# The handoff from a graph attention layer's projection to its first round: scores of the last row tile from W times a, the largest score inside the projection, the first parts dealt anew

## What is computed

```python
h = relu(layernorm(x)); x = x + _L0_gnn_ref(h, adj, adj)     # smoothing with a normalised adjacency
h = relu(layernorm(x)); x = x + _L1_gnn_ref(h, adj, W, a1, a2, W1, b1, ..., W4, b4)

def _L1_gnn_ref(x, adj, W, a1, a2, ...):                     # 8 heads of 64 features
    Wh = jnp.einsum('nf,hfd->hnd', x, W)
    e_src = jnp.einsum('hnd,hd->hn', Wh, a1)
    e_dst = jnp.einsum('hnd,hd->hn', Wh, a2)
    e = jax.nn.leaky_relu(e_src[:, :, None] + e_dst[:, None, :], 0.2)
    e = jnp.where(adj[None] > 0, e, -9e15)
    h = jax.nn.elu(jnp.einsum('hnm,hmd->hnd', jax.nn.softmax(e, axis=-1), Wh))
    ...                                                      # four dense layers, the last without relu
```

## Time and profile before

| | us |
|---|---|
| median of 3 runs | 876.22 (873.47 to 876.56) |
| profiled execution | 876.4 |
| its span, first to last instruction | 874.3 |
| busy: PE / DVE / ACT / POOL | 844.2 / 701.2 / 426.6 / 280.0 |
| granted TensorE clock, mean | 0.993 of full |

### The profile page before, as it was taken

How to read it: one execution, slowest core, us unless ns; L and a number is a source line. 1 busy time by engine, 2 the same in 40 slices (tenths; PEclk the granted TensorE clock), 3 DMA queues, 4 the chain that set the end, 5 groups by cost and what they waited for, 6 DMA issues and landing times.

```text
span 874.3 us, 15399 instructions
## 1 busy us (share of the span) xinstructions
PE 844.2 (97%) x5193; PEld 759.1 (87%) x5193; DVE 701.2 (80%) x1206; ACT 426.6 (49%) x781; POOL 280.0 (32%) x298
## 2 busy tenths in 40 slices
PE   2999999999999999999799999999999999998997
PEld 1888888888888888888699999999999999998876
DVE  6889986556556875586999999999999999999864
ACT  3445433321111111255576666666666666775653
POOL 0000000000000000076737555555555555565322
PEclk9999999999999999999899999999999999999999
DMA  9979932603223332050050000000000032000144
GB/s 349 406 259 351 366 96 71 193 0 120 96 96 97 96 96 72 1 193 3 28 221 15 22 24 27 26 24 24 25 26 25 24 97 68 19 1 1 49 145 147
DMA packets 36166, 87.39 MB, mean 100 GB/s; under 512 B 7120, under 2 KB 8016, under 8 KB 36112
## 3 DMA queue, kind: packets, MB, share of 16 engines
q1 hardware_dynamic: 35072, 82.46, 27.2%
q0 software_dynamic: 1040, 4.26, 1.3%
HBM read 73.93 MB, written 12.78 MB: 99 GB/s over the span
## 4 chain that ended last, share of the span: by engine, by line
PE 86%; DVE 11%; DMA 1%; ACT 1%; issue 1%; SPq 0%; DVEq 0%; ACTq 0%
PE bank L1660 22%; PE bank L77 16%; PE bank L79 16%; PE bank L78 16%; PE bank L1686 12%; DVE l_q L1249 8%; DMA l_kept<-adj 1%; PE bank L2185 1%; DVE wh L2057 1%; PE bank L929 1%; PE bank L2181 1%; PE bank L2182 1%; PE bank L2128 1%; DVE l_parts L1255 0%; DVE l_fine L1982 0%
## 5 line engine op out<-in xcount | busy, mean ns | idle before, releaser
L1249 DVE SCALAR_TENSOR_TENSOR l_q<-bank,neg_d,mask 128x512 fp32r<-128x512 f32 x512 | 338.8, 742 | 22.9 <-PE bank L1660 22.8
L1660 PE MATMUL bank<-l_parts,l_q 128*128 128x260 f32 x2048 | 252.5, 284 | 4.2 <-DVE l_q L1249 4.2
L1660 PEld LDWEIGHTS bank<-l_parts,l_q 128*128 128x128 f32 x2048 | 249.5, 190 | 4.9 <-issue 4.0
L77 PE MATMUL bank<-x_hi,s_hi 128*128 128x512 f32 x448 | 174.5, 389 | 0.0
L79 PE MATMUL bank<-x_hi,s_lo 128*128 128x512 f32 x448 | 174.3, 389 | 0.0
L78 PE MATMUL bank<-x_lo,s_hi 128*128 128x512 f32 x448 | 174.3, 389 | 0.0
L751 POOL TENSOR_TENSOR l_prod<-wh,l_a 128x512 f32<-128x512 f32 x30 | 36.2, 1228 | 385.0 <-ACT wh L723 385.0
L1415 ACT ACTIVATE l_mask<-mask 128x512 fp32r<-128x512 uint8 (+1 forms) x256 | 136.4, 620 | 0.1
L1686 PE MATMUL bank<-l_parts,l_mask 128*128 128x260 f32 x1024 | 127.2, 284 | 1.1 <-ACT l_mask L1415 1.1
L1686 PEld LDWEIGHTS bank<-l_parts,l_mask 128*128 128x128 f32 x1024 | 125.5, 189 | 1.3 <-ACT l_o_q L1421 1.3
L1421 ACT ACTIVATE l_o_q<-bank 128x260 f32<-128x260 f32 x128 | 49.5, 388 | 105.3 <-PE bank L1660 97.8
(11 more groups left out here) (204 smaller groups left out, 1117.4 us busy)
## 6 DMA issues: line engine op xcount, KB each, us to landing
rows<-adj_t SPq DMA_DIRECT2D x48, 512.0 KB, 3.8
l_now<-adj SPq DMA_DIRECT2D x16, 512.0 KB, 7.6
l_rows_k<-adj_t SPq DMA_DIRECT2D x16, 512.0 KB, 8.4
l_src<-e_rows SPq DMA_DIRECT2D x30, 256.0 KB, 3.1
l_kept<-adj SPq DMA_DIRECT2D x12, 512.0 KB, 13.0
wh_store<-wh POOLq DMA_DIRECT2D x1, 4160.0 KB, 15.8
l_h<-x SPq DMA_DIRECT2D x4, 1024.0 KB, 17.2
x<-x SPq DMA_DIRECT2D x1, 4096.0 KB, 13.9
```

Source lines behind the costliest of these rows:

```text
L77: pe.matmul(acc, hi, rhs_hi, start=first, stop=False, skip_group_check=True)
L1249: v.scalar_tensor_tensor(out=q[:, i, :], in0=bank[S_BANKS[hh]][:], scalar=neg_d[:, i, h:h + 1], in1=mask[:, i, cols], op0=ALU.is_ge, op1=A ...
L1660: return pe.matmul(bank[Q_BANKS[hh][t]][:, 0:PW], q[:, i, t * P:(t + 1) * P], parts[pair_slot][:, i, hh * PW:(hh + 1) * PW], start=i == 0, ...
```

## The change

It does the following, all between the second smoothing and the end of round 0.

- Scores of the last row tile. DVE forms `wa` = W times a, summed per head (128 x 4 x 16), during the second smoothing (`mix`: eight multiplies into `wh` as scratch, eight sums), and cuts it into hi and lo beside W. PE sums the last tile's scores from the cut features and `wa` (`sum_last_e`, 12 products of 16 columns) ahead of that tile's projection. Wh of that tile isn't used for scores any more.
- Largest score. PE's two products for it (turn of `tile_top`, spread of `top_w`) move into the last tile's projection, behind its second and third triple; the last tile's Wh is taken out of PSUM by ACT after the first two cuts (`last_wh`).
- Parts of the first round. DVE forms and subtracts the first A quarter; the third score copy moves behind the largest score (`third_scores`). ACT forms the second head's C cut in two halves, among the masks. Both second-head subtracts move from DVE to POOL (`second_rest`; C in two halves, then A), ahead of the transfer to `wh_store`. DVE's `second_cut` moves from q tile 8 of the second head to tile 4.
- Phases. In round 0 the first q phase goes tile by tile to its end, the M phase begins with banks 4 and 5 for four tiles, then banks 0 and 1, and the second half of the second head's parts is waited for at tile 8. PE's first two rounds are written out, and the loop of two runs once.

```diff
+            def mix(j):
+                n, k = j // KC, j % KC
+                if j == 0:
+                    v.wait_ge(w_loaded, 16 * (KC + 2))
+                if j < 2 * KC:
+                    v.tensor_tensor(wh[:, j, :, 0:HD], w_f[:, k, :, :], per_head(a_b[:, n, :]), ALU.mult
+                                    ).then_inc(w_chain, 1)
+                if j:
+                    n, k = (j - 1) // KC, (j - 1) % KC
+                    v.wait_ge(w_chain, 2 * j - 1 if j > 1 else 1)
+                    v.tensor_reduce(wa[:, k, n * H:(n + 1) * H], wh[:, j - 1, :, 0:HD], AX_X, ALU.add
+                                    ).then_inc(w_chain, 1)
             for s in range(2, G8):
                 cut(0, s // SLOTS, s % SLOTS)
+                mix(s - 2)
...
+                else:
+                    mix(s + 1)
             variances(0)
-            v.wait_ge(w_loaded, 16 * (KC + 2))
...
+                else:
+                    v.wait_ge(top_steps, 1)
+                    v.tensor_copy(e[:, t, :], bank[7][:, 0:2 * H]).then_inc(e_ready, 2)
+                    v.wait_ge(e_ready, 2 * t + 5)
+                    v.tensor_reduce(tile_top[:], d_m.rearrange("p t h -> p h t"), AX_X, ALU.max
+                                    ).then_inc(top_ready, 1)
+                    v.wait_ge(prod_ready, 2 * OWN + 2)
+                    reduce_part(OWN, OWN % 2, 0)
...
             def project(t, b):
                 pe.wait_ge(t_lo_ready, t + 1)
                 pe.wait_ge(wh_ready, t + 1)
+                if t == T - 1:
+                    sum_last_e(b)
                 for k in range(KC):
...
+                    if t == T - 1 and k == 1:
+                        pe.wait_ge(top_ready, 1)
+                        pe.transpose(bank[1][0:H, 0:P], tile_top[:], ident[:]).then_inc(top_steps, 1)
+                    if t == T - 1 and k == 2:
+                        pe.wait_ge(top_ready, 3)
+                        pe.matmul(bank[0][:, 0:H], top_w[:], ident[0:H, 0:H], start=True, stop=True
+                                  ).then_inc(top_steps, 1)
                 mm.then_inc(wh_summed, 1)
+            def sum_last_e(b):
+                pe.wait_ge(x1_done, T)
+                for k in range(KC):
+                    cols = slice(k * P, (k + 1) * P)
+                    mm = split_product(pe, bank[7][:, 0:2 * H], g_hi[:, b, cols], g_lo[:, b, cols],
+                                       wa_hi[:, k, :], wa_lo[:, k, :], k == 0)
+                mm.then_inc(top_steps, 1)
...
-                def second_rest(n):
-                    v.wait_ge(second_hi, n + 1)
-                    v.tensor_tensor(parts[0][:, :, of_head((C_LO, A_LO)[n], 1)], first_whole[2 + n],
...
-                choose(0, 0, 0, slice(0, QW), {G8: lambda: args_summed(v), T - QUAD: lambda: v.wait_ge(fac_ready, 1)})
+                quarter = slice(0, QUAD)
+                v.wait_ge(fac_ready, 1)
+                v.tensor_tensor(first_whole[0][:, quarter, :], wh[:, quarter, 0, :],
+                                fac["A"][:, quarter, 0:1].to_broadcast([P, QUAD, HE]), ALU.mult
+                                ).then_inc(chain, 1)
+                third_scores(v)
+                v.wait_ge(first_hi, 1)
+                v.tensor_tensor(parts[0][:, quarter, of_head(A_LO, 0)], first_whole[0][:, quarter, :],
+                                parts[0][:, quarter, of_head(A_HI, 0)].bitcast(F32), ALU.subtract
+                                ).then_inc(first_lo, 1)
...
-                choose(0, 0, 1, slice(0, QW), {2: lambda: second_rest(0), QUAD: lambda: late_args(v), G8: second_cut})
+                choose(0, 0, 1, slice(0, QW), {2: lambda: late_args(v), QUAD: second_cut})
...
+                a.wait_ge(wh_summed, WH_READY)
+                a.wait_ge(chain, 3)
+                cut_quarter(0, 0)
+                a.wait_ge(first_whole_ready, 1)
+                cut_quarter(0, 1)
+                last_wh(a)
...
+                for k in range(2):
+                    take_mask(0, 0, slice(0, QW), range(2) if k == 0 else range(2, 3))
+                    a.wait_ge(second_whole_ready, k + 1)
+                    half = slice(k * G8, (k + 1) * G8)
+                    a.activation(parts[0][:, half, of_head(C_HI, 1)], first_whole[2][:, half, :], ACT.Copy
+                                 ).then_inc(second_hi, 1)
+                take_mask(0, 0, slice(0, QW), range(3, QUAD))
                 take_q_sums(0, 0)
...
-                for n, ready in ((2, second_whole_ready), (3, late_whole_ready)):
-                    p.tensor_tensor(first_whole[n], wh[:, :, 1, :], fac["CA"[n - 2]][:, :, 1:2].to_broadcast([P, T, HE]),
-                                    ALU.mult).then_inc(ready, 1)
+                halves = (slice(0, G8), slice(G8, T))
+                for half in halves:
+                    p.tensor_tensor(first_whole[2][:, half, :], wh[:, half, 1, :],
+                                    fac["C"][:, half, 1:2].to_broadcast([P, G8, HE]), ALU.mult).then_inc(second_whole_ready, 1)
+                for k, half in enumerate(halves):
+                    p.wait_ge(second_hi, k + 1)
+                    second_rest(1, half)
+                p.tensor_tensor(first_whole[3], wh[:, :, 1, :], fac["A"][:, :, 1:2].to_broadcast([P, T, HE]),
+                                ALU.mult).then_inc(late_whole_ready, 1)
+                p.wait_ge(second_hi, 3)
+                second_rest(0, slice(0, T))
                 for b in range(2):
                     p.wait_ge(src_loaded[b], 16)
 
                 p.dma_start(wh_store.rearrange("(t p) f -> p t f", p=P),
                             wh[:].rearrange("p t h e -> p t (h e)")).then_inc(wh_stored, 16)
-                p.wait_ge(second_lo, 2)
+                p.wait_ge(second_lo, 3)
...
+                    at_start = isinstance(r, int) and r == 0
+                    if at_start:
+                        for tiles in ((0, 1), (2, 3)):
+                            for i in range(QUAD):
+                                pe.wait_ge(m_ready, made + i + 1)
...
-                    pe.wait_ge(second_lo, 2)
+                    pe.wait_ge(second_lo, 3)
                     q_phase(r, pair_slot, 1, also)
```

More of the change, by code:

```diff
@@ L752, in products @@
                                     ALU.mult).then_inc(prod_ready, 1)
-            p.wait_ge(w_ready, 1)
-            for t in range(T):
+            p.wait_ge(w_ready, 2)
+            for t in range(T - 1):
                 products(t, t % 2)
@@ L1181, in combine @@
             return first_head, second_head
[L1183 removed]
+        (programs, (third_scores, args_summed, late_args, last_wh, late_factors, late_scores), (src_spread, wh_summed, wh_ready, chain),
+         x1_stored, stored, fac_ready) = before
+        WH_READY = T + 2
         sync_before, vector_before, scalar_before, gpsimd_before, tensor_before = programs
@@ L1404, in fill_src, with take_mask @@
                     a.activation(bank[S_BANKS[hh]][:], src[:, hh, :], ACT.Copy).then_inc(src_filled, 1)
-                def take_mask(r, quad, cols):
-                    for i in range(QUAD * quad, QUAD * quad + QUAD):
+                def take_mask(r, quad, cols, tiles=range(QUAD)):
+                    for i in (QUAD * quad + n for n in tiles):
                         if i >= MR:
@@ L1661, in product @@
                                          parts[pair_slot][:, i, hh * PW:(hh + 1) * PW], start=i == 0, stop=i == T - 1)
-                    for i in range(T - QUAD):
+                    at_start = isinstance(r, int) and r == 0 and hh == 0
+                    for i in range(T if at_start else T - QUAD):
                         pe.wait_ge(q_ready, made + i + 1)
@@ L1687, in product @@
                                          parts[pair_slot][:, i, BOTH_C], start=i == 0, stop=i == T - 1)
-                    for i in range(T - QUAD):
+                    at_start = isinstance(r, int) and r == 0
+                    if at_start:
+                        for tiles in ((0, 1), (2, 3)):
+                            for i in range(QUAD):
+                                pe.wait_ge(m_ready, made + i + 1)
+                                for t in tiles:
+                                    if i == 0:
+                                        wait_for_bank(r, 1, t)
+                                    mm = product(t, i)
+                                if t == GT - 1:
+                                    mm.then_inc(m_done, 1)
+                    for i in range(QUAD if at_start else 0, T - QUAD):
                         pe.wait_ge(m_ready, made + i + 1)
+                        if at_start and i == G8:
+                            pe.wait_ge(second_lo, 2)
                         for t in range(GT):
@@ L1756, in _ @@
                 pe.wait_ge(first_lo, 2)
-                for hp in range(H // 2 - 1):
+                for r in range(2):
+                    sum_up(r, 0)
+                with pe.Fori(1, 2) as k:
+                    for b in range(2):
```

(2 more changed lines are left out.)

95 lines of the change are left out of this document (54 added, 41 removed).

## The result

The changed kernel takes 877.87 us (median of 9 runs, 877.03 to 879.01), the kernel before, beside it, 875.18 (9 runs, 873.47 to 876.56): a ratio of 1.0036, 95% interval 1.0026 to 1.0045. (The three runs known to the forecast, median 876.22, are among these nine.) The profiled execution took 879.01, its span is 877.1. So the change costs some 2.7 us, though it does all that it says: scores, q tiles and masks come earlier. The loss arises in one place, on POOL.

A forecast was written before the change was run, and what follows sets the result against it. The projection-to-attention seam was taken to bound, by when PE enters its unbroken run; the 2.4 us on offer are lost as POOL's 3.0 less 0.75 slack makes PE 2.3 late: 876.4 + 2.3 = 878.7, less 0.2, 878.5; range 877.8 to 879.8.

The forecast's parts named there:

- Handoff: From projection to attention: arguments from 421.8, 2.7 us earlier; DVE starts q at 424.0 against 425.20, gaining 1.2.
- On offer: Round 1's M phase could start at 460.8 instead of 463.26, 2.4 us earlier, with ACT's masks the bound.
- POOL: Subtracts moved to POOL ahead of its transfer to wh_store put that issue at 440.85, 3.0 us later.
- upper bound of 4.5: Largest delay of the wh_store issue, if ACT's queue is a microsecond late and DVE's with it.
- the second gate: PE's phase after round 1's M phase waits for ACT's M banks, behind POOL's next-pair product; PE 2.3 us late.
- the first: Round 1's third and fourth M products wait for banks 0 and 1 until 463.6; the 2.4 us on offer are gone.
- slack of 0.75: At PE's phase after round 1's M phase: second M bank free at 470.65, needed at 471.4.
- A: Rival: the wh_store transfer doesn't gate, PE's run begins at 460.8, 2.4 us gained, 873.8; chance 0.17.
- D: Rival: faster by over 0.5%; neither masks nor POOL gate, DVE's 459 counts with a little more, 871.6; chance 0.04.
- E: Rival: the handoff hop ends no sooner, q starts at 425.2, POOL's list is 1.2 later, 879.7; chance 0.08.
- B: Rival: without DVE's subtract beside its issue, the wh_store transfer lands up to 1.16 us sooner, 877.3; chance 0.14.
- C: Rival: slower by over 0.5%; POOL's queue slips further, passing 4.4 us at an issue after 443.0; chance 0.10.

The follow-up runs named there:

- SP's issue: Changed kernel, but SP and not POOL issues the transfer to wh_store, behind round 1's source rows: 871.47 us, ratio 0.9956.
- the clock held up: Changed kernel with 28 repeated products ahead of round 1's M phase, to fill PE's wait: 878.79 us, ratio 1.0040.
- the issue a little earlier: Changed kernel with DVE's two small steps moved to q tile 6, 875.75 us, or POOL's issue moved ahead of its last subtract, 872.58 us.
- the subtract twice: Changed kernel with POOL's last second-head subtract done twice ahead of the transfer's issue: 877.50 us, ratio 1.0033.
- four times: Changed kernel with POOL's last second-head subtract done four times ahead of the transfer's issue: 882.42 us, ratio 1.0078.
- `late_args` later: Changed kernel with DVE's two small steps for factors B and D at the second head's q tile 6, not 2: 875.75 us, ratio 1.0002.
- subtracts on DVE with SP's issue: Changed kernel with SP issuing the transfer and both second-head subtracts given back to DVE: 871.69 us, ratio 0.9965.

## Why the prediction was right

878.5 was forecast and 877.87 measured, by the mechanism forecast: POOL's subtracts put the transfer off, and PE's earlier start is lost at its gates.

- **Handoff.** The 12 narrow products ran from 417.59 to 418.93, 0.11 each, as costed by the transposes; the last quarter of parts was whole at 431.45 (431.6, whose working the forecast doesn't show); arguments at 421.92 (421.8 forecast), q at 423.99 (424.0), q phase over at 435.24 (435.2). Nothing in the second smoothing stalled.
- **On offer.** Round 0's M phase ended at 444.68, 0.7 before the forecast, and round 1's could start at 460.42 (460.8). ACT's masks are the bound there, as said: PE's wait of 1.32 for L1470 stands in the changed kernel and in those with SP's issue and POOL's subtracts alike.
- **POOL.** Its A product ended at 437.88 (437.9). The mis-sized term is what follows: DVE's cast was put at 438.6, "DVE waits 0.3, with slack behind it", and ended at 439.89, as the small step ahead of it was held for some 1.6 us beside POOL's product. No price was set on that. The issue came 4.3 late, not 3.0: near the upper bound of 4.5, which stood for another cause.
- **The gates.** The sum had the second gate as the last wait, some 2 us long, with the first opening at 463.6 without loss. Both are real, but the first is the one seen in the changed kernel: PE's third product starts at 464.28 after a wait of 3.45, and the half clock behind it covers the second. With the clock held up, or the issue a little earlier, the second shows (1.81, 1.80, 1.26) as forecast.
- **The size.** 2.3 was forecast for PE; its lag is 3.3 (shifted), the time's 2.7. The missing 1.0 is the late cast: with the issue's own 4.05 (shifted) in place of 3.0, the forecast's slack of 0.75 leaves 3.3, though the way there is the first gate and the slow clock (2.9 with the clock held up). That 878.5 lies only 0.6 from 877.87 is partly luck: it was built on a median of 876.22, and nine runs gave 875.18, so the base was 1.0 too high where the loss was too small.
- **Rivals.** A (the store doesn't gate) falls in the changed kernel and is what the kernels on SP show, with more than its 2.4: the M phase begins 2.95 earlier there (460.43 against 463.38, both shifted) and the time gains 4.4; the lowest times differ by 3.46, which puts most of the other 1.4 down to executions that differ outside the seam; no run shows it. D's 871.6 is reached by those kernels, not by the changed one, and not by D's way: ACT's masks hold their M phase at 460.4, where D needed 459. E falls with the arguments at 421.92. B (the transfer lands sooner) gained 0.27 of its 1.16: 15.99 to 15.72. So taking the subtract off DVE gave little, and the rule cited there, as it was applied to this subtract, isn't borne out. Whether the source rows' packets run among the transfer's goes with more, 1.35. C was priced wrongly: an issue at 444.47 costs no more than one at 442.14, and 0.5% is passed only between that and 449.06.

## What to carry to other kernels

When work moves to an idle engine, look at what that engine issues or releases behind it: here a subtract of 2.2 us, and the 2.1 us that POOL waited for its input, ahead of a transfer cost more than all early work gained; with that subtract behind the issue PE's next phase came 4.8 us sooner. A transfer's landing and not its engine's busy time tells how much idle time an engine has to give. Where two gates stand a microsecond apart, removing one shows the other, so cost both.

## What the runs showed of the hardware

- **Small DVE steps held by POOL.** A `TENSOR_SCALAR` of 128 columns took 0.21 to 0.23 with POOL idle, and 1.87, 1.88, 1.19 or 1.17 when begun while POOL multiplied or subtracted; each of these ended within 0.1 us of POOL's instruction (437.96 against 437.88). The step that began 0.03 to 0.05 behind POOL's product by the record (L954, 435.84 against 435.79) took its 0.21 unheld, and that product 2.07 to 2.09, where it takes 1.96 to 1.99 with no such step at its start. The q tiles, 0.66 each, with one operand in PSUM, ran through. The Trainium skill (SBUF — State Buffer, section Who interferes with whom) states that `tensor_scalar` in a two-port mode and a GpSimd instruction exclude each other for the whole length of the one that came first; the held steps agree, and which of the two came first in L954's case the record doesn't tell.
- **The transfer's length.** 4160 KB took 14.1 and 14.2 from issue to landing on POOL's queue with the source rows already landed (the kernels with the subtract twice and four times), 15.4 to 16.0 in the six others that issue it there.
- **PE's clock.** It fell behind waits of 3.45 (to 0.50), 3.70 (0.65 over 464 to 468) and, in the kernel with four subtracts, 4.30 us (0.50 over 448 to 454; 128 products in 18.28, not 15.9); behind waits of 1.26 to 2.10 it stayed at 1.00; behind the one of 2.4 near the end it did either (next item). In the handoff, where the kernel before had 0.83, the changed kernel has 1.00 from 416 to 435, but those with 28 products, the doubled and the fourfold subtract have 0.86, 0.87 and 0.92 over 425 to 435, with no edit that early.
- **Open.** Near the end of attention PE waits 2.41 to 2.44 us for DVE in all twelve kernels. From the end of that wait the rest of the last q phase takes 3.5 us in three (`late_args` later, four times, and subtracts on DVE with SP's issue), where the clock stays at 1.00, and 4.9 to 5.0 in the other nine, where it falls. PE's rows in the changed kernel, and in the one with `late_args` later:

```profile
806.79 0.63 PE L2231 MATMUL bank<-ident,wh 128*128 128x128 f32 x4 [2.43 <-DVE l_enc_t_lo L2120]
...
808.35 3.45 PE L1737 MATMUL bank<-l_parts,l_q 128*128 128x260 f32 x16
```

```profile
804.74 0.63 PE L2231 MATMUL bank<-ident,wh 128*128 128x128 f32 x4 [2.43 <-DVE l_enc_t_lo L2120]
...
806.05 2.18 PE L1737 MATMUL bank<-l_parts,l_q 128*128 128x260 f32 x16
```

The kernels don't differ there, and which of them keep the clock follows no edit. No run was made on its cause. It adds up to 1.5 us to some of the times above, which is why smaller differences between them are read from the traces alone.
